# A mixer layer on one core: routing weights spread by DMA and multiplied in by GpSimd, score maxima woven in by fours

## The chip, the cores and the metric

The kernel runs on one core of one Trainium2 chip. The metric is the time of one execution on the device in microseconds; lower is better. Before the change it is 1653.61 us, the median of three runs (1653.0 to 1655.18).

## The reference

x has 8 sequences of 1024 tokens with 256 features. The layer normalizes x (no affine part), gives the result to two branches, and adds both to x:

```
xn  = layernorm(x)
out = x + attention(xn) + experts(xn)

attention: 16 heads of 16; heads 0..3 see every earlier token, heads 4..15 the last 64
    w = softmax(mask(q @ k.T * 16**-0.5));  ctx = w @ v;  out = ctx @ w_out + b_out

experts, once forward and once "inverse" (8 experts of rank 64 each), with Q and K projections of xn:
    xV = Q V;  yW = K W;  prod = xV * cumsum(yW over tokens)
    weights = softmax(gelu(Q @ r1.T + b1) @ r2.T + b2 + expert_bias)        # 8 weights per token
    out = (sum over experts of (prod * weights) @ U.T + weights @ b) / (position + 1)
out = (forward + alpha * inverse) @ W_O.T
```

All inputs and the output are float32. The product of three factors, `xV * weights * cumsum(yW)`, is what the change rearranges.

## The kernel before

**Work.** The 8 sequences are cut into 16 chunks of 512 tokens, `ch` = 0 to 15. Even chunks are the first half of a sequence, odd ones the second half, whose global heads see twice the keys. Features stand on the 128 partitions and tokens in the free dimension. Float32 matmuls are made from split operands: a value is a high part that TensorE takes, plus the rest (`XH`, `XL`; `CH`, `CL` for the running sums over tokens; `PH`, `PL` for the products; `WH`, `WL` for weights), so one product is three passes.

**Order.** A planner (`Plan`) writes one list of stages by hand-made rules. Each engine's program walks the whole list and issues its own part of each stage in that order, with semaphores between the engines; `uses=` gives a stage its turn on a PSUM bank or buffer. SP issues all DMAs, in the same order. A stage thus waits in every engine's queue behind all stages ahead of it in the list.

**The expert stage of a chunk.** Both branches together are eight blocks of 128 rows (two experts each), j = 0 to 7. For each block:

1. `x` (TensorE, line 587 through `mms`): six matmuls of 512 columns into bank 2. ScalarE copies bank 2 to `prod[:, j % 3]` (line 993).
2. `c`: the same from the running sums into bank 3.
3. `product`: TensorE spreads the routing weights of the two experts over 64 partitions each. It is one matmul of the 0/1 matrix `spread[:, j, :]` with `WT` (99 rows: the weights cut into three bfloat16 parts, by tokens) into bank 4 (line 701). VectorE multiplies `prod` by bank 4 (line 1273), then by bank 3 (line 1276). ScalarE rounds the result to `PH` (line 1003) and GpSimd subtracts it to get `PL` (line 1446).
4. `mix` (line 714): eight matmuls of 256 columns with `PH` and four with `PL`, into banks 0 and 1, which collect the output of the whole chunk. `open` (line 675) starts them with the bias terms.

`expert_groups` orders the groups: x(j+1), then c(j) with product(j), then mix(j-1). Into them `weave` sets the maxima of the attention scores, which the softmax of this chunk needs. `peak_groups` lists 12 local maxima (`lpeak`, one mask matmul at line 726 and eight small ones at line 732) and 10 or 26 global ones (`gpeak`, lines 743 and 746). It adds `found` (VectorE cuts the maxima into bfloat16 parts), `rows` (TensorE turns the local ones, ScalarE copies them out, SP stores and reloads them) and nine pieces of the next chunk's layernorm on VectorE. Each maximum is read from its bank by VectorE (lines 1197 and 1204). Before the change the list is cut into groups of two, and the maxima take turns on banks 5, 6 and 7.

**The stages behind it.** The local stage: scores of the twelve local heads, with the next chunk's transposes (`turn`), running sums (GpSimd, into `CH` and `CL`, from `rest`) and parts of q and k (through `rest` as well). The parts go out to DRAM and come back rearranged (`stacks`, local heads first, lines 1502 and 1523; global heads at line 1525). The global stage: scores of the four global heads, with the next chunk's x(0), c(0), router (`hidden`, `logits`), `gates` and `gate_parts`, where VectorE forms the weights `gate[:, 2]` (line 1255) and their three parts, and the values (`values`, then `vshift` by DMA). `weight_rows` turns the parts into `WT`. After it come x(1) and x(2) of the next chunk, around the turning of the context (`cparts`), then `finish`: 24 matmuls of the output projection (line 856), VectorE adds the residual in two halves (`xt`, line 1306) and SP stores the chunk (line 1560). SP then waits for that store before it loads the next residual (line 1494). Local scores take their bank by line 766, the first matmul behind the expert stage.

## Time and profile before

| | us |
|---|---|
| median of 3 runs | 1653.61 |
| the profiled execution | 1654.62 |
| its span, first to last instruction | 1652.9 |
| TensorE busy | 1563.5 |
| VectorE busy | 937.7 |
| ScalarE busy | 684.4 |
| GpSimd busy | 284.2 |

The profile is of one execution. Times within it are microseconds from the start of the span. Busy times of TensorE are modelled, since matmuls overlap in the array; a row's mean duration (0.39 us for a matmul of 512 columns) is thus longer than what it adds to a sequence (0.23 us), which the chain shows. The chain is the work that ended last, followed back step by step to what released it. DMA figures are the packets of the core's 16 DMA engines; the share of a queue is the packets' time over 16 engines times the stretch, and can pass 100% a little, where packets overlap. The granted TensorE clock was 0.996 of full speed.

### The profile page before, as it was taken

The numbers are of one execution on the slowest core, as the hardware profiler recorded it, in microseconds if no ns is written. First come the engines' busy times: TensorE is split into PE (matmuls) and PEld (weight loads), VectorE is DVE, ScalarE is ACT, GpSimd is POOL, SyncE is SP. The second block draws the span as 40 slices with busy tenths as digits, with TensorE's granted clock in tenths as the row PEclk, the third lists the DMA queues.
The fourth block names the chain that finished last, engine by engine and source line by source line (L and its number), as shares of the span: only waits on it lengthen the run. The fifth ranks groups of instructions, "written<-read, shape, count | busy, mean of one in ns | idle before, by whom it ended". The sixth has DMA issues, their size and how long they took to land.

```text
span 1652.9 us, 36914 instructions
## 1 busy us (share of the span) xinstructions
PE 1563.5 (95%) x15489; PEld 1112.8 (67%) x15489; DVE 937.7 (57%) x2048; ACT 684.4 (41%) x1224; POOL 284.2 (17%) x346
## 2 busy tenths in 40 slices
PE   5899999999999999999999999999999999999997
PEld 4576675767757676676757767576675767667674
DVE  6665672737537484564837567274763748447461
ACT  3426245261543517243362523626254351634425
POOL 2011121211112111121201212021111201112111
PEclk9999999999999999999999999999999999999999
DMA  8514417072350906218071350806326080530800
GB/s 207 63 31 88 80 34 123 10 117 51 76 89 4 151 15 104 61 38 130 4 122 45 77 91 21 125 21 106 62 64 100 4 139 27 96 69 23 132 4 14
DMA packets 128186, 116.48 MB, mean 70 GB/s; under 512 B 19251, under 2 KB 127668, under 8 KB 127972
## 3 DMA queue, kind: packets, MB, share of 16 engines
q1 hardware_dynamic: 128020, 114.12, 38.5%
q8 instruction: 122, 2.00, 0.6%
q14 instruction: 44, 0.36, 0.1%
HBM read 73.43 MB, written 34.34 MB: 65 GB/s over the span
## 4 chain that ended last, share of the span: by engine, by line
PE 76%; DVE 14%; ACT 5%; issue 4%; POOL 1%; DMA 0%; DVEq 0%; ACTq 0%; POOLq 0%
PE PS L587 33%; PE PS L714 8%; DVE block_peak L1204 4%; PE PS L793 3%; PE PS L825 3%; PE PS L732 3%; PE PS L856 3%; PE PS L766 3%; PE PS L807 3%; PE PS L772 3%; DVE prod L1273 2%; PE PS L726 2%; DVE prod L1276 2%; ACT HE L1029 2%; PE PS L746 2%
## 5 line engine op out<-in xcount | busy, mean ns | idle before, releaser
L1446 POOL TENSOR_TENSOR PL<-prod,PH 128x512 fp32r<-128x512 f32 x128 | 164.5, 1285 | 792.7 <-ACT PH L1003 792.7
L1003 ACT ACTIVATE PH<-prod 128x512 fp32r<-128x512 f32 x128 | 80.8, 631 | 428.8 <-DVE prod L1276 428.8
L587 PE MATMUL PS<-XH,WH 128*128 128x512 f32 x512 | 220.4, 430 | 4.5 <-DVE XL L1145 1.9
L587 PE MATMUL PS<-XH,WL 128*128 128x512 f32 x512 | 203.6, 398 | 0.0
L587 PE MATMUL PS<-XL,WH 128*128 128x512 f32 x512 | 203.2, 397 | 0.0
L1204 DVE TENSOR_REDUCE block_peak<-PS 128x4 f32<-128x512 f32 x288 | 186.9, 684 | 4.2 <-PE PS L746 4.2
L993 ACT ACTIVATE prod<-PS 128x512 f32<-128x512 f32 x128 | 76.3, 596 | 231.3 <-PE PS L587 220.3
L1029 ACT ACTIVATE HE<-PS 128x512 f32<-128x512 f32 (+1 forms) x320 | 159.7, 552 | 26.1 <-PE PS L807 23.5
L1197 DVE TENSOR_REDUCE peak<-PS 128x4 f32<-128x512 f32 x192 | 125.6, 685 | 41.0 <-PE PS L732 41.0
L1273 DVE TENSOR_TENSOR prod<-PS,prod 128x512 f32<-128x512 f32 x128 | 88.1, 689 | 104.6 <-PE PS L701 104.6
L714 PE MATMUL PS<-UH,PH 128*128 128x256 f32 x512 | 139.5, 306 | 0.0
L1439 POOL TENSOR_SCALAR_AFFINE_SELECT HE<-HE 128x256 f32<-128x256 f32 x128 | 50.7, 409 | 478.9 <-ACT HE L1029 476.4
L1286 DVE RECIPROCAL cinv<-PS 128x16 f32<-128x16 f32 x64 | 16.3, 254 | 205.2 <-PE PS L837 205.2
L714 PE MATMUL PS<-UL,PH 128*128 128x256 f32 x512 | 126.0, 280 | 0.0
L587 PE MATMUL PS<-CH,WH 128*128 128x512 f32 x256 | 109.2, 427 | 9.1 <-DVE prod L1276 9.0
L587 PEld LDWEIGHTS PS<-XH,WH 128*128 128x128 f32 x512 | 96.9, 189 | 26.6 <-DVE WL L1341 2.2
L1021 ACT ACTIVATE HE<-PS 128x512 f32<-128x512 f32 x192 | 104.6, 596 | 21.5 <-PE PS L772 21.5
L587 PEld LDWEIGHTS PS<-XH,WL 128*128 128x128 f32 x512 | 96.7, 189 | 23.1
L807 PE MATMUL PS<-area 99*128 99x256 bf16 (+1 forms) x640 | 100.4, 267 | 7.8 <-ACT HE L1029 3.9
L587 PEld LDWEIGHTS PS<-XL,WH 128*128 128x128 f32 x512 | 97.3, 190 | 14.6
L746 PE MATMUL PS<-area 96*128 96x128 bf16 x1152 | 100.8, 220 | 5.8 <-DVE block_peak L1204 4.9
L807 PEld LDWEIGHTS PS<-area 99*128 99x128 bf16 x640 | 41.8, 98 | 93.5 <-ACT HE L1029 56.9
(195 smaller groups left out, 3154.8 us busy)
## 6 DMA issues: line engine op xcount, KB each, us to landing
parts_d<-area SPq DMA_DIRECT2D x32, 768.0 KB, 5.1
area<-parts_d SPq DMA_DIRECT2D x128, 192.0 KB, 12.4
area<-parts_d SPq DMA_DIRECT2D x32, 576.0 KB, 12.5
tok<-in_L_attn_x_dram SPq DMA_DIRECT2D x16, 512.0 KB, 6.5
xt<-in_L_attn_x_dram SPq DMA_DIRECT2D x16, 512.0 KB, 3.9
out_dram<-xt SPq DMA_DIRECT2D x16, 512.0 KB, 3.7
area<-parts_d SPq DMA_DIRECT2D x96, 64.0 KB, 5.9
Vs<-Va SPq DMA_DIRECT2D x24, 204.0 KB, 7.6
```

What stands on the lines that cost most here:

```text
L587: ins = e.matmul(ps, a, b, start=first and k == 0, stop=last and k == n - 1, skip_group_check=True)
L714: ins = e.matmul(out_half(t), (PH, PL)[part][:, h, t * P:(t + 1) * P], u[:, j, :], start=False, stop=False, skip_group_check=True)
L746: ins = e.matmul(psum(i, lo=P * g, hi=P * (g + 1)), QS[0:G16, g, t * P:(t + 1) * P], KG[0:G16, g, j * P:(j + 1) * P], start=(g == 0 and no ...
L807: ins = e.matmul(psum(i, lo=HALF * a + lo, hi=HALF * (a + 1)), KG[0:KSTK, g, j * P:(j + 1) * P], QS[0:KSTK, g, half * HALF + lo:(half + 1) ...
L993: e.activation(prod[:, j % 3, :], psum(2), ACT.Copy).then_inc(bank_read[2])
L1003: e.activation(PH[:, h, :], prod[:, j % 3, :], ACT.Copy).then_inc(phi)
L1021: e.activation(HE[:, k, :], psum(i), ACT.Exp, scale=SCALE).then_inc(bank_read[i])
L1029: e.activation(two(HE[:, k, :], lo), two(psum(i), lo), ACT.Exp, scale=SCALE).then_inc(bank_read[i])
L1197: e.tensor_reduce(peak[:, t, NG + 4 * grp:NG + 4 * (grp + 1)], psum(i).rearrange("p (a k) -> p a k", a=4), AX_X, ALU.max).then_inc(bank_re ...
L1204: e.tensor_reduce(block_peak[ch % NC][:, t, :, j], psum(i).rearrange("p (a k) -> p a k", a=4), AX_X, ALU.max).then_inc(bank_read[i])
L1273: e.tensor_tensor(prod[:, r, :], psum(4), prod[:, r, :], ALU.mult).then_inc(bank_read[4])
L1446: e.tensor_tensor(PL[:, j % 2, :], prod[:, j % 3, :], PH[:, j % 2, :].bitcast(F32), ALU.subtract).then_inc(plo)
```

## The change

The weights no longer go through TensorE's spread. `gate_parts` gets a VectorE transpose of 32x32 blocks of `gate[:, 2:4]` into `weights_t`. SP writes it to DRAM as `weights_d` (16 rows of 512 tokens, float32) in four DMAs. For each block j a stage `wide` reads two rows of it, each 64 times, into one of three buffers of 128 x 512 float32 (two of them are `rest`). A stage `weigh` on GpSimd multiplies `prod` by it, before `product`. wide(j + 3) is issued behind weigh(j). Bank 4 so becomes free of the spread, and the maxima take turns on banks 4 to 7 and are cut into groups of four. `spread`, its selects and its memset are gone. `WT` stays for the bias terms.

```diff
@@ peak_use
-        return f"bank{(5, 6, 7)[turns['peak'] % 3]}"
+        return f"bank{4 + turns['peak'] % 4}"
@@ expert_groups
-                order.append([(add_x, ch, j + 1, part) for part in range(2)])
+                order.append([(add_x, ch, j + 1, part) for part in range(2)] + [(add_weigh, ch, j + 1)])
@@ planner
     def add_product(ch, j):
-        add("product", ch, j, uses=["bank4"])
+        add("product", ch, j)
+    def add_weigh(ch, j):
+        add("weigh", ch, j)
+        if j + WIDE < 2 * KB:
+            add_wide(ch, j + WIDE)
+    def add_wide(ch, j):
+        add("wide", ch, j, uses=[f"wide{j % WIDE}"])
+    def add_gate_parts(ch):
+        add("gate_parts", ch)
+        for j in range(WIDE):
+            add_wide(ch, j)
@@ peak_groups
-        return [order[n] + (order[n + 1] if n + 1 < len(order) else []) for n in range(0, len(order), 2)]
+        return [[stage for group in order[n:n + 4] for stage in group] for n in range(0, len(order), 4)]
@@ behind the global stage (weigh(0), (1), (2) of the next chunk around x(1), cparts, x(2))
+            add_weigh(ch + 1, 0)
             run([(add_x, ch + 1, 1, part) for part in range(2)])
+            add_weigh(ch + 1, 1)
...
             run([(add_x, ch + 1, 2, part) for part in range(2)])
+            add_weigh(ch + 1, 2)
@@ TensorE
-                elif kind == "product":
-                    e.matmul(psum(4), spread[:, j, :], WT[:, :], start=True, stop=True).then_inc(w_ps)
@@ VectorE, turn (rest is also a buffer of wide)
+                        q.wait_ge(weighed, nth("weigh", ch - 1, 6 + k))
@@ VectorE, gate_parts
+                    q.wait_ge(weights_out, 16 * 4 * ch)
+                    e.transpose(weights_t[:, :].rearrange("p (t w k) -> p t w k", t=T, w=2),
+                                gate[:, 2:4].rearrange("p w t k -> p t w k")).then_inc(weights_turned)
+                    q.wait_ge(weights_turned, ch + 1)
@@ VectorE, product
-                    q.wait_ge(w_ps, nth(*stage))
-                    e.tensor_tensor(prod[:, r, :], psum(4), prod[:, r, :], ALU.mult).then_inc(bank_read[4])
+                    q.wait_ge(weighed, nth("weigh", ch, j))
                     q.wait_ge(c_ps, nth(*stage))
                     e.tensor_tensor(prod[:, r, :], psum(3), prod[:, r, :], ALU.mult).then_inc(bank_read[3])
@@ GpSimd
+                elif kind == "weigh":
+                    q.wait_ge(bank_read[2], use("bank2", "x", ch, j, 0))
+                    q.wait_ge(wide_in[j % WIDE], 16 * use(f"wide{j % WIDE}", "wide", ch, j))
+                    e.tensor_tensor(prod[:, j % 3, :], prod[:, j % 3, :], wide[j % WIDE], ALU.mult).then_inc(weighed)
@@ SP
+                elif kind == "gate_parts":
+                    q.wait_ge(weights_turned, ch + 1)
...
+                    for g in range(4):
+                        e.dma_start(weights_d.rearrange("k (t g r) -> g k t r", t=T, g=4)[g],
+                                    weights_t[32 * g:32 * g + 2 * KE, :].rearrange("k (t r) -> k t r", t=T)).then_inc(weights_out, 16)
+                elif kind == "wide":
+                    q.wait_ge(weights_out, 16 * 4 * (ch + 1))
+                    if j >= WIDE:
+                        q.wait_ge(weighed, nth("weigh", ch, j - WIDE))
...
+                    e.dma_start(wide[j % WIDE], weights_d[2 * j:2 * j + 2, :].unsqueeze(1).to_broadcast([2, R, C])).then_inc(wide_in[j % WIDE], 16)
```

## Rows read from the trace of the kernel before

**Rows 1.** The page: part 1, and the first line of part 4 (the chain).

```profile
PE 1563.5 (95%) x15489; PEld 1112.8 (67%) x15489; DVE 937.7 (57%) x2048; ACT 684.4 (41%) x1224; POOL 284.2 (17%) x346
...
PE 76%; DVE 14%; ACT 5%; issue 4%; POOL 1%; DMA 0%; DVEq 0%; ACTq 0%; POOLq 0%
```

**Rows 2.** Busy time by stretch, one pair of chunks: us, then busy us (instructions) of each engine, clock, DMA share, GB/s.

```profile
370.81:567.97 197.16, 189.99 (x1920) 135.75 (x1921) 112.76 (x248) 83.18 (x149) 34.68 (x41) 1.00 0.39 70
```

**Rows 3.** The chain through a second half: start us, us, what.

```profile
373.88 0.26 DVE xt L1306
...
374.49 0.69 DVE prod L1273
...
377.62 0.23 PE PS L701
...
385.87 0.32 PE PS L726
386.19 0.34 PE PS L732 x8
386.54 1.60 PE PS L587 x6
...
393.28 1.32 DVE stats L1118 x4
...
404.88 0.45 PE PS L746 x8
...
407.25 1.45 PE PS L587 x6
...
422.46 0.39 PE PS L766
```

**Rows 4.** The chain through a first half.

```profile
283.20 0.26 DVE xt L1306
...
325.94 0.38 PE PS L766
```

**Rows 5.** Groups by line: busy us, mean ns, then idle before.

```profile
L1446 POOL TENSOR_TENSOR PL<-prod,PH 128x512 fp32r<-128x512 f32 x128 | 164.5, 1285 | 792.7 <-ACT PH L1003 792.7
...
L1273 DVE TENSOR_TENSOR prod<-PS,prod 128x512 f32<-128x512 f32 x128 | 88.1, 689 | 104.6 <-PE PS L701 104.6
```

**Rows 6.** DMA packets, 340 to 346 us (parts_d<-area, one store of 768 KB).

```profile
DMA packets 784, 0.79 MB, mean 131 GB/s; under 512 B 16, under 2 KB 784, under 8 KB 784
...
q1 hardware_dynamic: 784, 0.79, 39.0%
```

**Rows 7.** DMA packets, 394 to 395.6 us (peak_d_local<-peak_f alone, 36 KB).

```profile
DMA packets 48, 0.04 MB, mean 23 GB/s; under 512 B 12, under 2 KB 48, under 8 KB 48
```

**Rows 8.** DMA packets, 395.6 to 400 us (area<-peak_d_local alone, 36 KB).

```profile
DMA packets 7, 0.05 MB, mean 12 GB/s; under 512 B 3, under 2 KB 3, under 8 KB 3
...
q1 hardware_dynamic: 6, 0.04, 3.5%
```

**Rows 9.** DMA packets, 4 to 7 us (the first loads).

```profile
q1 hardware_dynamic: 542, 0.93, 80.8%
```

**Rows 10.** SP's DMA issues in order of time: start us, us, what.

```profile
394.34 0.33 SPq L1553 DMA_DIRECT2D peak_d_local<-peak_f  x1
395.81 0.26 SPq L1555 DMA_DIRECT2D area<-peak_d_local  x1
```

**Rows 11.** VectorE in order of time, gates before a second half.

```profile
359.31 0.22 DVE L1255 TENSOR_TENSOR gate<-gate,gsum 128x64 f32<-128x64 f32 x1
```

**Rows 12.** DMA queue, 360 to 366 us.

```profile
q1 hardware_dynamic: 788, 0.77, 117.8%
```

**Rows 13.** VectorE in order of time, gates before a first half.

```profile
457.02 0.23 DVE L1255 TENSOR_TENSOR gate<-gate,gsum 128x64 f32<-128x64 f32 x1
```

**Rows 14.** Busy time by stretch, the last full one of that DMA load.

```profile
464.00:466.00 2.00, 2.00 (x21) 1.44 (x21) 0.00 (x0) 1.02 (x3) 0.77 (x2) 1.00 1.19 121
```

**Rows 15.** Busy time by stretch, chunk 0.

```profile
85.00:90.00 5.00, 5.00 (x48) 2.92 (x47) 3.36 (x6) 1.54 (x3) 0.24 (x1) 1.00 0.81 158
```

More of the change, by code:

```diff
@@ L316, in mixer_layer @@
         add_on("fold_u", n, uses=[fold_use()])
-    add("gate_parts", 0)
+    add_gate_parts(0)
     for part in range(2):
         add_x(0, 0, part)
+    add_weigh(0, 0)
     for part in range(2):
@@ L359, in mixer_layer @@
             order = order[1:]
-            side = [[(add_gates, ch + 1)], [(add, "gate_parts", ch + 1)]] + [[]] * (2 * (ch % NC))
+            side = [[(add_gates, ch + 1)], [(add_gate_parts, ch + 1)]] + [[]] * (2 * (ch % NC))
             side += [[(add_values, ch + 1, 0)], [(add_values, ch + 1, 1)]]
@@ L391, in mixer_layer @@
         bias_rows = sb("bias_rows", [KSTK, D], BF16)
-        spread = sb("spread", [KSTK, 2 * KB, P], BF16)
         W2 = sb("W2", [P, DB, KE])
@@ L428, in mixer_layer @@
         rest = sb("rest", [P, 2, C])
+        weights_t = sb("weights_t", [P, T * 32])
+        wide = [rest[:, 0, :], rest[:, 1, :], sb("wide2", [P, C])[:, :]]
         carry = sb("carry", [P, DB])
@@ L511, in mixer_layer @@
         logits_ps, gate_max, gate_exp, gate_split, gate_turned = (sem(n) for n in ("logits_ps", "gate_max", "gate_exp", "gate_split", "gate_turned"))
-        x_ps, c_ps, w_ps, phi, plo = (sem(n) for n in ("x_ps", "c_ps", "w_ps", "phi", "plo"))
+        x_ps, c_ps, phi, plo = (sem(n) for n in ("x_ps", "c_ps", "phi", "plo"))
+        weights_turned, weights_out, weighed = (sem(n) for n in ("weights_turned", "weights_out", "weighed"))
+        wide_in = [sem(f"wide{i}_in") for i in range(WIDE)]
         lpeaks_ps, gpeaks_ps, lscores_ps, gscores_ps, ctx_turned, ctx_hi, out_ps = (
@@ L695, in tensor_program @@
                         ins.then_inc(c_ps)
-                elif kind == "product":
-                    ch, j = key
-                    q.wait_ge(bank_read[7], use("bank7", "weight_rows", ch))
-                    take(4, *stage)
-                    e.matmul(psum(4), spread[:, j, :], WT[:, :], start=True, stop=True).then_inc(w_ps)
                 elif kind == "mix":
@@ L1105, in vector_program @@
                         e.memset(view, 0.0).then_inc(blank)
-                    for view in (ident, ident_b, peak_mask_l, peak_mask_g, spread, mask_l):
+                    for view in (ident, ident_b, peak_mask_l, peak_mask_g, mask_l):
                         e.memset(view[:], 0.0).then_inc(cleared)
@@ L1270, in vector_program @@
                     r = j % 3
-                    q.wait_ge(bank_read[2], use("bank2", "x", ch, j, 0))
-                    q.wait_ge(w_ps, nth(*stage))
-                    e.tensor_tensor(prod[:, r, :], psum(4), prod[:, r, :], ALU.mult).then_inc(bank_read[4])
-                    q.wait_ge(bank_read[4], use("bank4", *stage))
+                    q.wait_ge(weighed, nth("weigh", ch, j))
                     q.wait_ge(c_ps, nth(*stage))
@@ L1408, in gpsimd_program @@
                     select(peak_mask_l[0:64, 1, :], [[1, P]], -WINDOW, 0, after=7)
-                    for n, first in enumerate((0, 3 * HD, 5 * HD)):
-                        view = spread[:, :, :].rearrange("r j (a m) -> r (j a) m", a=2)
-                        select(view, [[-1, 4 * KB], [0, R]], -first, 1, ALU.not_equal, 1.0, after=8 + n if n else 0)
                     select(mask_l[:, :], [[-1, WINDOW]], 0, 1)
-                    select(mask_l[:, :], [[1, WINDOW]], WINDOW, -1, after=12)
+                    select(mask_l[:, :], [[1, WINDOW]], WINDOW, -1, after=9)
                     e.iota(positions[:, :], pattern=[[P, ST]], base=1, channel_multiplier=1).then_inc(selected)
@@ L1555, in sync_program @@
                     e.dma_start(QS[G16:KSTK, lo:lo + n, :], peak_d[which].rearrange("(a h) t -> a h t", h=n)).then_inc(peak_in[which], 16)
+                elif kind == "gate_parts":
+                    ch, = key
+                    q.wait_ge(weights_turned, ch + 1)
+                    for i in range(WIDE):
+                        q.wait_ge(wide_in[i], 16 * (use(f"wide{i}", "wide", ch, i) - 1))
+                    for g in range(4):
+                        e.dma_start(weights_d.rearrange("k (t g r) -> g k t r", t=T, g=4)[g],
+                                    weights_t[32 * g:32 * g + 2 * KE, :].rearrange("k (t r) -> k t r", t=T)).then_inc(weights_out, 16)
+                elif kind == "wide":
+                    ch, j = key
+                    q.wait_ge(weights_out, 16 * 4 * (ch + 1))
+                    if j >= WIDE:
+                        q.wait_ge(weighed, nth("weigh", ch, j - WIDE))
+                    elif j == 2:
+                        q.wait_ge(weighed, nth("weigh", ch - 1, 5))
+                    else:
+                        q.wait_ge(part3, nth("parts", ch, 0, DB - 1))
+                        q.wait_ge(clo, DB * (ch + 1))
+                        if ch == 0:
+                            q.wait_ge(bias_in, 16 * 15)
+                    e.dma_start(wide[j % WIDE], weights_d[2 * j:2 * j + 2, :].unsqueeze(1).to_broadcast([2, R, C])).then_inc(wide_in[j % WIDE], 16)
                 elif kind == "finish":
```

9 lines of the change are left out of this document (5 added, 4 removed).

## The prediction

> **What bounds the kernel now.** First the page's busy table and its chain: TensorE is busy for 95% of the span and carries 76% of the chain, VectorE 14% [rows 1]. Then the busy time by stretch: chunks come in pairs, a first and a second half of a sequence, and each pair takes 197.2 us with 190 us of TensorE, the DMA engines 0.39 busy on the mean [rows 2]. Then the chain through one chunk. F is the moment at which the last matmul of `finish` of the chunk before has ended. In a second half the chain leaves F at 373.9, goes over VectorE (`xt`, then `prod` twice) back to TensorE, where each L701 (the spread) costs 0.23, and reaches the first local score at 422.5, F+48.6 [rows 3]. In a first half it takes from 283.2 to 325.9, F+42.8 [rows 4]. This "expert stage", eight experts woven with the maxima, is what the change touches; the local and global stages behind it stay. So TensorE bounds, with VectorE close behind it in the second halves. DMA has 0% of the page's chain [rows 1], so its rows have to be looked up for themselves: the change makes eight DMAs per chunk a condition of the products.
>
> **What goes.** 128 spread matmuls at 0.23 on the chain [rows 3]: 29.4 us of TensorE, 1.84 per chunk. 128 VectorE multiplications of 0.69 (88 us) [rows 5], which lie partly in the chain: at a chunk's start one stands between `xt` and c(1) [rows 3]. Bursts of four on four banks switch weights less often and spare some 0.3 to 0.6 us per chunk (six matmuls after local maxima take 1.60, after global ones 1.45, else 1.40 [rows 3], and half as many such places remain; back-to-back bursts pay 0.1 of it). The memset and three selects at the start are beside the first loads and cost nothing.
>
> **What comes on engines.** 128 GpSimd multiplications, priced by the subtraction of the same three operands, 1.285 [rows 5]. GpSimd then works 2.6 us per expert of 5 to 6 us, and is idle otherwise in this stage. The order counts though: weigh(j+1) stands in GpSimd's queue before the subtraction PL(j), and mix(j) waits for PL(j). If weigh(j+1) waits for its rows, so does mix(j). One VectorE transpose per chunk lies in the gate stage, where VectorE idles: nothing. `rows` now takes bank 4 amid a burst; in a second half it waits for VectorE's read of a maximum that stands behind the layernorm moments (1.32 for their first part, 1.9 with all of it [rows 3]), 2.6 us with the maxima themselves; in a first half the next maximum waits for ScalarE's copy of `rows`, 0.85 (both estimates).
>
> **What comes on the DMA engines, the step that decides.** Each `wide` writes 128 partitions of 2 KB, 256 KB, from a source whose outermost count is 2 (two rows, each repeated 64 times). How many engines carry one DMA can be read from its completion packets. The store of the parts, 128 partitions, shows 784 packets in its window, 768 of data and 16 under 512 B [rows 6]. The store of the local maxima, 36 rows, shows 48 packets, of which 12 are small [rows 7]. The load behind it, 36 rows taken as 3 by 12, shows 6 packets on the kernel's queue, 3 small and 3 of data [rows 8]. So 128 went over 16 engines, 36 over 12, an outermost 3 over 3. No row shows a DMA whose sides differ, as a `wide` has 2 at its source and 128 at its target: by the source it goes over 2 engines, by the target over 16. I take 2, since a part that goes to one engine must be whole on both sides, and keep 16 as a rival. The Trainium skill ("DMA: Bandwidth & Descriptors", Why a DMA increments its semaphore by 16 and not by 1) has a rule for it: the largest count up to 16 that divides the slowest dimension of both patterns, always on the lowest-numbered engines. By that rule a `wide` has 2, and always the same two; the trace's 16, 12 and 3 agree with it, and no run here shows the mixed case yet.
>
> The price of one `wide` on its two engines is 131 KB per engine. One engine moved 0.79 MB/(0.390 x 6.0 us x 16) = 21.1 GB/s in packets of 1 KB [rows 6], 0.93/(0.808 x 3.0 x 16) = 24.0 in the first loads, with packets of 3 KB among them [rows 9], and 37 KB/(0.035 x 4.4 x 16) = 15 in the 12 KB packets into single partitions [rows 8]. That gives 6.2, 5.5 and 8.7 us. A packet of 2 KB is nearest to the first two: I take 23 GB/s, 5.7 us, and keep 5.2 to 8.7. Eight are 46 us per chunk on those two engines, in a stage that takes 42.8 or 48.6, and each engine serves its DMAs in order, so that the others stand in the same line. A landing costs 1.5 us from issue on top: the store of the maxima is issued at 394.3 and the load that waits for it at 395.8 [rows 10].
>
> The line on the two engines, second half (F = 373.9). The weights are ready after L1255, at 359.5 [rows 11]; the DMA engines are full with the local stacks until 366 (117.8% busy) [rows 12], and the four weight DMAs stand behind them. So the first `wide` starts at F-6.4, three end at F+10.7. Vs and the global stacks (1.18 MB, 74 KB per engine at 21 GB/s, 3.5 us) then stand behind them: F+14.2. wide 3 to 5, issued after weigh 0 to 2: F+31.3. The store of the output stands behind wide 5 in SP's program, which waits for weigh(2): F+32.8, landed F+34.3. SP then waits for that landing before the next residual load, and wide 6 and 7 stand behind this load in the program: load to F+36.7, wide 7 to F+48.1, landed F+49.6, weigh(7) F+50.9, PL(6) F+52.2, mix(6) F+53.7. Before: 48.6. Loss 5.1.
> First half (F = 480.3). The weights are ready at 457.2 [rows 13] and land once the local stacks are through, at 466 (1.19 busy until then [rows 14]): three wides from F-13.0 to F+4.1, Vs and stacks F+7.5, wide 5 F+24.6, store landed F+27.6, load F+30.0, wide 7 F+41.4, landed F+42.9, mix(6) ends F+47.0. Before: 42.8. Loss 4.2.
> Seven such pairs (chunks 1 to 14): 7 x 9.3 = 65 us. Chunk 0: its DMA engines are busy until about 90 (0.81 from 85 on [rows 15]); eight wides end at 136.1, mix(6) at 141.7, where now the stage ends at 128.8: 13. Chunk 15 has a third of its experts in the local stage and loses nothing. The sum is 78 us on the profiled execution's 1654.6 (span 1652.9 and 1.7 around it; the median of the runs is 1653.6, 1.0 lower): 1733. TensorE's savings are inside this: it waits them out.
>
> **Rivals.** (1) All 16 engines carry a `wide`, and it lands 2.3 us after its issue (262 KB at 16 x 21 GB/s, and 1.5 on top), long before its product; then TensorE bounds on. Its work in a second half, by the pieces of rows 3: 19 groups of x, c and mix at 1.40, `open` 0.54, spreads 1.84, 12 local maxima (0.66 each, 0.34 and 0.32) with their switches 8.5, 26 global ones (0.225 each, a mask for four) with theirs 7.5, `rows` 0.2: 45.2, so 3.4 of the 48.6 are waits for VectorE. The spreads and these waits go, 0.65 of switches too, and 2.6 for `rows` comes: 3.3 faster. First half: 41.1 of work and 1.7 of waits; 1.84, 0.5 and 1.6 go, 1.05 comes: 2.9. Seven pairs: 43 us, 1611; with the spreads alone 1625. For it: the trace has room (0.39); against it: the counts of rows 7 and 8. (2) Two engines, but 26 GB/s each (5.0 us): 0.7 x 8 = 5.6 less per chunk than in the sum, over 15 chunks 84: 1733 becomes 1649, and 1620 to 1650 if the line of DMAs is also shorter than I count. The point at which the sign turns is thus 5.0 us per `wide`. For it: 24.0 of rows 9 is a mean over many DMAs, with gaps; against it: that the rows read have been written just before, all 64 times from the same place. (3) 15 GB/s, as in rows 8: 3 us more for each of eight in 15 chunks, 360: 2093; 1913 for half of that. For it: it is the one load over few engines that the trace has; against it: its packets are six times longer and go to one partition each. (4) GpSimd and VectorE block one another. Both already run side by side 128 times with 1.285 and 0.69 as unchanged means [rows 5]; I give it nothing of its own.
>
> **How the numbers follow.** Forecast (1733, own range 1655 to 1860) 0.69; rival 1 0.14; rival 2 0.08; rival 3 0.09. A change under 0.2% (3 us) could not be told from none here. Faster: rival 1 and three quarters of rival 2, 0.20; same 0.03; slower 0.77. The range 1630 to 1890 leaves out rival 1 and the far part of rival 3.
>
> **What would show it.** The small packets per `wide`: 2, not 16; issue to landing 7 us alone and 10 to 25 in the stage; GpSimd's weigh waiting for DMAs, above all 6 and 7; TensorE waiting for PL at L714, its busy share under 92%, the maxima of VectorE long done; an expert stage of 54 and 47 us. Wrong if a `wide` lands in 3 to 4 us with 16 small packets: then stages of 45.3 and 39.9 and rival 1's time.

## The result and the profile after

The changed kernel takes 1852.9 us (median of 4 runs, 1847.2 to 1854.9); the kernel before, run beside it, 1654.4. The ratio is 1.119, 95% interval 1.117 to 1.121: slower by 198 us, where 78 were forecast. The direction held; the size did not.

The page of the changed kernel, part 1, the TensorE clock and the chain, beside [rows 1]:

```profile
PE 1604.6 (87%) x15361; PEld 1156.5 (62%) x15361; DVE 871.6 (47%) x1935; ACT 681.2 (37%) x1224; POOL 441.2 (24%) x471
...
PEclk9989899998989889898998989989899998989989
...
q1 hardware_dynamic: 149780, 148.20, 38.0%
...
PE 55%; DMA 25%; DVE 10%; SPq 2%; ACT 2%; POOL 2%; issue 2%; POOLq 0%; ACTq 0%; DVEq 0%
...
out_dram<-xt SPq DMA_DIRECT2D x16, 512.0 KB, 15.4
```

TensorE's share of the chain fell from 76% to 55%, and DMA's rose from 0 to 25%. The chain's next line puts 16% of the span on `wide` and 8% on the store of the weights. TensorE is busy 1604.6 us. The instructions of before less the 128 spreads make 1563.5 - 29.4 = 1534.1. The surplus is 70.5 us; most of it is the same work at a lower clock, as e6 and e18 below show. The output's store lands 15.4 us after its issue; before it took 3.7.

One pair of chunks, beside [rows 2]; 222.0 us where it was 197.2, at a mean granted clock of 0.92:

```profile
531.60:753.60 222.00, 195.92 (x1903) 141.02 (x1902) 104.58 (x234) 82.82 (x148) 54.74 (x57) 0.92 0.39 81
```

The DMA share is 0.39 in both. No mean over sixteen engines shows two that are full. What does is the packet count, in the way of [rows 6 to 8]. Here is the queue from 656 to 662 us, where only the transfers of `wide` move bytes and one of them ends (the output's store is issued in it, and its packets of 1 KB come later):

```profile
DMA packets 145, 0.29 MB, mean 49 GB/s; under 512 B 2, under 2 KB 2, under 8 KB 145
...
q1 hardware_dynamic: 145, 0.29, 13.0%
```

There are two packets under 512 B, and the share is 13.0% of sixteen engines, which is 2.08 of them: a `wide` runs on two engines. The pages' counts of packets under 512 B say the same of all chunks together: 24627 here and 28467 in e1, 3840 more, which is 256 transfers with 16 for 128 with 2. In the whole trace the packets of 2 KB have a median of 84 ns and a mean of 94, that is 5.4 to 6.0 us for the 64 on each engine.

GpSimd's multiplications through a second half (F = 631.5), in order of time, with the two subtractions behind the third. In brackets is what GpSimd waited for, and how long:

```profile
638.37 1.26 POOL L1461 TENSOR_TENSOR prod<-prod,rest 128x512 f32<-128x512 f32 x1 [16.68 <-DMA rest<-weights_d]
644.45 1.26 POOL L1461 TENSOR_TENSOR prod<-prod,rest 128x512 f32<-128x512 f32 x1 [4.82 <-DMA rest<-weights_d]
652.27 1.26 POOL L1461 TENSOR_TENSOR prod<-prod,wide 128x512 f32<-128x512 f32 x1 [6.56 <-DMA wide<-weights_d]
653.49 2.50 POOL L1466 TENSOR_TENSOR PL<-prod,PH 128x512 fp32r<-128x512 f32 x2
661.41 1.28 POOL L1461 TENSOR_TENSOR prod<-prod,rest 128x512 f32<-128x512 f32 x1 [5.42 <-DMA rest<-weights_d]
...
671.29 1.28 POOL L1461 TENSOR_TENSOR prod<-prod,rest 128x512 f32<-128x512 f32 x1 [5.11 <-ACT prod L1009]
...
690.89 1.30 POOL L1461 TENSOR_TENSOR prod<-prod,rest 128x512 f32<-128x512 f32 x1 [4.30 <-DMA rest<-weights_d]
```

weigh(0) runs at F+6.9 and weigh(2) at F+20.8. Directly behind weigh(2) come two subtractions, PL(0) and PL(1). The list has weigh(0), (1) and (2) ahead of the first `product`, so PL(0), and with it mix(0), stands in GpSimd's queue behind the third multiplication. For weigh(4) and (5) GpSimd waits for ScalarE, for weigh(7) again for a transfer. SyncE's issues of the same stretch show why the first comes so late:

```profile
605.05 6.83 SPq L1543 DMA_DIRECT2D area<-parts_d  x8
617.52 2.54 SPq L1583 DMA_DIRECT2D weights_d<-weights_t  x4
630.65 1.10 SPq L1598 DMA_DIRECT2D rest<-weights_d  x2
631.79 2.79 SPq L1598 DMA_DIRECT2D wide<-weights_d  x1
634.68 5.53 SPq L1556 DMA_DIRECT2D Vs<-Va  x1
...
641.46 7.42 SPq L1545 DMA_DIRECT2D area<-parts_d  x8
648.92 4.53 SPq L1598 DMA_DIRECT2D rest<-weights_d  x2
...
657.88 5.20 SPq L1603 DMA_DIRECT2D out_dram<-xt  x1
673.26 0.40 SPq L1514 DMA_DIRECT2D xt<-in_L_attn_x_dram  x1
```

The local stacks are issued from 605.1 and the four small stores of the weights from 617.5; the stores land at 630.6, F-0.9. With two-engine transfers under way, single issues take 2.8 to 5.5 us of SyncE where [rows 10] have 0.3.

TensorE over that stretch. The columns are: us, then busy us (instructions) of PE, PEld, DVE, ACT and POOL, granted clock, DMA share, GB/s:

```profile
625.00:636.00 11.00, 8.84 (x78) 6.61 (x76) 2.89 (x5) 2.17 (x4) 0.00 (x0) 1.00 0.43 55
636.00:641.00 5.00, 0.59 (x2) 0.50 (x2) 1.34 (x3) 0.61 (x1) 1.26 (x1) 0.50 0.14 48
641.00:646.00 5.00, 5.00 (x28) 2.77 (x26) 2.00 (x4) 0.02 (x1) 1.26 (x1) 0.50 0.60 151
...
651.00:656.00 5.00, 1.19 (x5) 1.20 (x6) 0.00 (x0) 0.00 (x0) 3.71 (x3) 0.50 0.15 46
656.00:661.00 5.00, 5.00 (x34) 2.72 (x32) 1.21 (x2) 0.60 (x1) 0.00 (x0) 0.61 0.13 49
```

TensorE stood still for 6.3 us ahead of c(1) and for 4.3 ahead of the part of mix(0) that takes PL(0), and from 636 to 656 the clock is granted at 0.50, the 1.2 GHz level. Its waits, summed over the kernel, each with the number of times and the longest:

```profile
PE PS L731 <- POOL PL L1466: 98.3, 15, 7.5
PE PS L610 <- DVE prod L1294: 55.4, 16, 9.1
PE PS L774 <- DVE block_peak L1221: 22.1, 8, 3.0
```

The prediction had the first kind (PL, late through `wide`) and the third (`rows` on bank 4: 2.76 us each, estimated 2.6). In the pair shown, the expert stage of the second half takes 64.4 us (forecast 53.7), that of the first half 52.1 (forecast 47.0, [rows 4] 42.8). The 48.6 that the prediction read for a second half before [rows 3] goes to the second matmul of line 766. To the first, as the 64.4 is measured, it is 47.8 (TensorE in order of time, F = 373.9):

```profile
421.66 0.39 PE L766 MATMUL PS<-mask_l,ident_b 128*128 128x512 bf16 x1
```

The two stages thus lose 16.6 and 9.3 us, 25.9 a pair, where the windows have 24.8.

### The profile page after: what moved, and what is told of

Same layout as the page of the kernel before. It is cut to its first block, busy times and chain, and to the rows that moved or that the text cites. A ratio compares the mean times of both kernels' runs of the same rounds, so it can differ in the third digit from the quotient of the medians.

```text
span 1853.2 us, 36905 instructions
## 1 busy us (share of the span) xinstructions
PE 1604.6 (87%) x15361; PEld 1156.5 (62%) x15361; DVE 871.6 (47%) x1935; ACT 681.2 (37%) x1224; POOL 441.2 (24%) x471
## 2 busy tenths in 40 slices
DMA packets 149947, 150.56 MB, mean 81 GB/s; under 512 B 24627, under 2 KB 133044, under 8 KB 149732
## 4 chain that ended last, share of the span: by engine, by line
PE 55%; DMA 25%; DVE 10%; SPq 2%; ACT 2%; POOL 2%; issue 2%; POOLq 0%; ACTq 0%; DVEq 0%
PE PS L610 25%; DMA wide<-weights_d 16%; DMA weights_d<-weights_t 8%; PE PS L731 8%; DVE block_peak L1221 4%; PE PS L810 3%; PE PS L789 2%; PE PS L783 2%; PE PS L749 2%; PE PS L743 2%; PE PS L763 2%; PE PS L928 2%; SPq L1583 2%; DVE tok L1154 1%; PE PS L854 1%
## 5 line engine op out<-in xcount | busy, mean ns | idle before, releaser
L1461 POOL TENSOR_TENSOR prod<-prod,rest 128x512 f32<-128x512 f32 x96 | 122.9, 1280 | 517.7 <-DMA rest<-weights_d 387.5
L610 PE MATMUL PS<-XH,WH 128*128 128x512 f32 x512 | 226.5, 442 | 4.5 <-DVE XL L1161 1.9
L610 PE MATMUL PS<-XH,WL 128*128 128x512 f32 x512 | 212.6, 415 | 0.0
L610 PE MATMUL PS<-XL,WH 128*128 128x512 f32 x512 | 211.9, 414 | 0.0
L731 PE MATMUL PS<-UH,PL 128*128 128x256 f32 x512 | 89.4, 300 | 98.3 <-POOL PL L1466 98.3
L610 PE MATMUL PS<-CH,WH 128*128 128x512 f32 x256 | 118.4, 462 | 55.4 <-DVE prod L1294 55.4
L731 PEld LDWEIGHTS PS<-UH,PL 128*128 128x128 f32 x512 | 74.9, 204 | 101.4 <-POOL PL L1466 101.4
L731 PE MATMUL PS<-UH,PH 128*128 128x256 f32 x512 | 132.9, 293 | 0.0
L610 PEld LDWEIGHTS PS<-XL,WH 128*128 128x128 f32 x512 | 102.7, 201 | 15.7
L610 PE MATMUL PS<-CL,WH 128*128 128x512 f32 x256 | 108.2, 423 | 0.0
## 6 DMA issues: line engine op xcount, KB each, us to landing
out_dram<-xt SPq DMA_DIRECT2D x16, 512.0 KB, 15.4
```

The lines of the kernel that those rows point to most:

```text
L610: ins = e.matmul(ps, a, b, start=first and k == 0, stop=last and k == n - 1, skip_group_check=True)
L731: ins = e.matmul(out_half(t), (PH, PL)[part][:, h, t * P:(t + 1) * P], u[:, j, :], start=False, stop=False, skip_group_check=True)
L1461: e.tensor_tensor(prod[:, j % 3, :], prod[:, j % 3, :], wide[j % WIDE], ALU.mult).then_inc(weighed)
```

## The experiments

Two theories at first. The two-engine transfers cost the time, by the line on their rings as the prediction laid it out, only longer. Against it: the way over two engines (GpSimd, then VectorE), the maxima on four banks, or TensorE's clock carry a good part by themselves. All ratios are to the kernel before, run beside each. "Maxima" gives how they are woven in (pairs or fours) and on how many banks; "`wide` on" is the number of DMA engines of one transfer.

| kernel | `wide` on | maxima | us | ratio, 95% |
|---|---|---|---|---|
| before | – | pairs, 3 banks | 1654 | 1 |
| the change | 2 | fours, 4 | 1852.9 | 1.119 [1.117, 1.121] |
| e1 | 16 | fours, 4 | 1661.3 | 1.004 [1.002, 1.006] |
| e2 | 16 | pairs, 3 | 1652.5 | 0.999 [0.998, 1.001] |
| e3 | 2 | pairs, 3 | 1837.2 | 1.110 [1.107, 1.113] |
| e4 | – | fours, 3 | 1685.3 | 1.019 [1.017, 1.021] |
| e8 | 16 | fours, 3 | 1684.1 | 1.018 [1.016, 1.020] |
| e10 | 16 | pairs, 4 | 1676.0 | 1.015 [1.012, 1.019] |
| e14 | 4 | fours, 4 | 1720.3 | 1.042 [1.038, 1.045] |
| e15 | 16 first 3, 2 last 5 | fours, 4 | 1661.5 | 1.005 [1.003, 1.007] |
| e16 | 2 first 3, 16 last 5 | fours, 4 | 1860.9 | 1.125 [1.123, 1.128] |
| e18 | 16, TensorE filled | pairs, 3 | 1641.6 | 0.992 [0.990, 0.993] |

### The two parts of the change, taken apart

e1, `wide` on sixteen engines; nothing else moves but the semaphore's count (32 for 16):

```diff
-e.dma_start(wide[j % WIDE], weights_d[2 * j:2 * j + 2, :].unsqueeze(1).to_broadcast([2, R, C]))
+for h in range(2):
+    e.dma_start(wide[j % WIDE][R * h:R * (h + 1), :], weights_d[2 * j + h:2 * j + h + 1, :].to_broadcast([R, C]))
```

> The changed kernel with each `wide` transfer cut into two, one for each of its two source rows, so that the outermost dimension of each is 64 destination partitions and no longer 2 source rows; same bytes, same waits. If the loss comes from the transfers running on two of the sixteen DMA engines, this kernel lands a `wide` in about a microsecond and falls to what the first rival of the prediction gave, 1611 us, or up to 10 us above, as the stores of the weights still land only at the end of `finish`. If what costs is the way of the product over GpSimd (VectorE and GpSimd in a row where one engine was) or the maxima on four banks, it stays above 1750. If it is the clock of TensorE alone, which fell in the waits on those transfers, it also goes, as the waits go: this kernel does not tell that apart.

1661.3 us. The two engines are worth 191.6 of the 198 us, so the way over GpSimd is not what costs them. But 1661 is not the 1611 of the prediction's first rival.

e2 puts the maxima back on top of e1, e3 on top of the change:

```diff
-return f"bank{4 + turns['peak'] % 4}"
+return f"bank{(5, 6, 7)[turns['peak'] % 3]}"
-return [[stage for group in order[n:n + 4] for stage in group] for n in range(0, len(order), 4)]
+return [order[n] + (order[n + 1] if n + 1 < len(order) else []) for n in range(0, len(order), 2)]
```

> The kernel with the `wide` transfers on sixteen engines, and the maxima woven in by pairs on banks 5, 6 and 7, as before the change: the spreading alone. The prediction's sum for this was 1625 us, that is 14 us more than with the fours. If the fours and their wait on bank 4 cost something rather than save it, this one is at or under the time of its neighbour with the fours.

> The changed kernel as it is with two-engine transfers, but the maxima by pairs on banks 5, 6 and 7: the first half of the change alone. If the transfers set the time, the order of the maxima changes little: 1853 us within 15. If the maxima on four banks have a good part in the loss of 198 us, it falls below 1800.

1652.5 and 1837.2. Fours on four banks cost 9 us with sixteen engines and 16 with two, where the prediction's 1625 and 1611 had them save 14. The spreading alone on sixteen engines equals the kernel before; I had given 1625. The tie is a balance: in e2's profiled run the stage of a first half takes 39.7 us (before 42.8) and that of a second half 50.3 (before 47.8). Here and below, such a pair of numbers without a chunk is the mean of the seven first or second halves among chunks 1 to 14, by the timelines of TensorE.

e4 has the last two lines of that diff reversed in the kernel before, which makes its pairs fours; e8 does the same to e2. e10 has e2 on banks 4 to 7.

> The kernel before, with the maxima woven in by fours, still on banks 5, 6 and 7 (bank 4 is taken by the spread weights there): the second half of the change without its fourth bank. Four maxima in a row on three banks make TensorE wait for VectorE's reduction once in each group: I expect 1654 us plus 0 to 15. A rival, that longer stretches of one kind of work save changes in the order and so TensorE time, gives 1645.

> The spreading on sixteen engines with the maxima by fours on banks 5, 6 and 7, without the fourth bank. On the kernel before, this step cost 31 us, and TensorE's wait for the maxima's reductions 37 us. If the fourth bank is what makes fours bearable, this gives 1652 plus 25 to 35; if the cost on the kernel before came from VectorE being busier there (128 products more), under 1665.

> The spreading on sixteen engines, maxima by pairs, but on banks 4 to 7: the fourth bank without the fours. With fours on four banks the time was 1661, with pairs on three 1652.5, with fours on three 1684. If bank 4 costs because `rows` uses it too (TensorE waited 22 us there in second halves and 5.5 in first), this gives 1665 to 1675. If the fours are what costs and a fourth bank only ever helps, it gives 1652 or a few us less.

Fours on three banks cost 31 us, both on the kernel before and on e2. e4 came out above its expectation. These are TensorE's waits there for the reductions of the maxima, which were 4.9 and 0.6 us in the kernel before:

```profile
PE PS L746 <- DVE block_peak L1204: 36.9, 46, 1.5
...
PE PS L726 <- DVE peak L1197: 9.2, 17, 0.6
```

The fourth bank alone costs 23 (e10), where TensorE waits 17.5 us ahead of `rows` for VectorE's read of bank 4, and 5.5 behind `rows`. The two together cost 9. So the fourth bank takes most of the fours' wait away, and on four banks the fours are 15 us faster than pairs (e1 against e10). `rows` on the same bank is the wait that stays, 22.1 and 5.5 us in e1; that it is the whole price was not shown. e7 tried to take that wait away too, by putting `rows` two maxima later in second halves:

```diff
-gpeaks[2].append((add_rows, ch, 0))
+gpeaks[4 if c else 2].append((add_rows, ch, 0))
```

> The whole change with `wide` on sixteen engines (1661.3 us), and in second halves the `rows` of the local maxima two maxima later, so that the bank 4 that it takes was last used three maxima ahead and not one. TensorE's 8 waits there, 22.1 us in all, should go: 1639 to 1645 us. If VectorE, which is late with the maxima, is itself the bound of that stretch, the wait only moves to the next maximum and the time stays at 1661.

1658.0 us, with 10 runs spread from 1651 to 1669, so the gain of 3 on e1 is not shown. In its profiled run, the longest of the ten, the wait for VectorE was gone and that of the next user of bank 4 for ScalarE's copy had grown:

```profile
PE PS L763 <- ACT peak_f L1031: 23.1, 16, 2.4
```

In e1 the same row has 5.5 us (8 times, at most 0.7). The wait moved, as the second sentence of the expectation had it, though not to VectorE.

### Where in the chunk the two engines cost

e14 keeps the packets but spreads each `wide` over four engines (e1's two DMAs, with the source as `to_broadcast([4, R // 4, C])`):

> The whole change with each `wide` cut in two, with an outermost dimension of four in each: the packets are the same 128 of 2 KB, on four DMA engines instead of two, 32 on each. By 84 to 94 ns a packet that is 2.7 to 3.0 us a transfer, and 22 to 24 us a chunk on these rings instead of 43 to 48. If the loss comes from how long a `wide` fills its rings, it halves or better against sixteen engines (1661): 1670 to 1720. If what matters is only that a few rings are more loaded than the rest and everything that spans all sixteen waits for them, it is still above 1750.

1720.3 us: 59 above sixteen engines, where two have 192. Twice the engines leave a third of the loss. e15 and e16 split the eight transfers of a chunk by `j < 3` and `j >= 3`:

```diff
+for h in range(2 if j < 3 else 1):
+    if j < 3: (e1's transfer of one row)
+    else: (the change's transfer of both rows)
```

> The whole change with the first three `wide` of each chunk on sixteen engines and the five others on two. TensorE's long waits in the changed kernel are those for the first two products of a chunk (98 us at mix(0) and 55 at c(1)), and the first three `wide` are what is late there. If the loss of 192 us against sixteen engines is theirs, this gives 1661 plus 20 to 50: 1695. If it is the line of the five others that sets the stage, 1800 or more.

> The counterpart: the first three `wide` of each chunk on two engines, the five others on sixteen. If the first three carry the loss, this gives 1853 less 10 to 50: 1820. If it is the line of the five others, 1720 or less. Were the two parts independent, the gains of this kernel and of its counterpart would add up to 192 us; if the losses overlap, so that either group alone is enough to be late, they add up to less.

1661.5 and 1860.9 us, and both expectations had the first three carry less. This is the sharpest pair of the study: with the first three on sixteen engines the loss is gone to the last microsecond, though five of eight still run on two; with only the first three on two it is all there. That e16 is 8 us above the changed kernel is not explained. GpSimd in e15, in a second half with F = 577.9:

```profile
580.59 2.64 POOL L1466 TENSOR_TENSOR prod<-prod,rest 128x512 f32<-128x512 f32 x2 [12.53 <-DMA rest<-weights_d]
583.19 1.30 POOL L1466 TENSOR_TENSOR prod<-prod,wide 128x512 f32<-128x512 f32 x1
...
595.02 1.29 POOL L1466 TENSOR_TENSOR prod<-prod,rest 128x512 f32<-128x512 f32 x1 [7.44 <-DMA rest<-weights_d]
...
604.04 1.28 POOL L1466 TENSOR_TENSOR prod<-prod,rest 128x512 f32<-128x512 f32 x1 [6.50 <-ACT prod L1014]
...
624.26 1.29 POOL L1466 TENSOR_TENSOR prod<-prod,rest 128x512 f32<-128x512 f32 x1 [4.04 <-DMA rest<-weights_d]
```

weigh(2) is at F+5.3 rather than F+20.8, and the stage ends at F+51.6. That is 46 us behind weigh(2); in the changed kernel the end is 43.6 behind it. The rest of a second half takes its 44 to 46 us whichever engines carry transfers 3 to 7, and 43.6 in e16 too. The reason that the third transfer counts, and not only the first, stands in GpSimd's queue: PL(0) waits behind weigh(2). No run put PL(0) ahead of it, so what that would give back is not known. e12 says the same of the piece of the line that I had counted with most care, the residual's load between `wide` 5 and 6. It moves this load behind `wide` 7:

> The changed kernel with the load of the residual (which waits for the landing of the output's store, 15.4 us after its issue as it stands behind two-engine transfers) moved behind the last `wide` of the chunk in SyncE's queue. In the profiled chunk SyncE sat in that wait from 657.9 to 673.3 while `wide` 6 could have been issued at about 661. If that wait is on the path, each second half gains 5 to 8 us and each first half some: 1853 less 50, so 1803 within 15. If the two engines are busy in that time anyway with the output's store and `wide` 5, so that `wide` 6 would land no earlier, 1845 or more.

1850.4 us (ratio 1.119 [1.117, 1.121]): nothing. The 15 us that SyncE spends from the issue of that store to its landing are off the path.

### Why the first product is late

Three ways to get the small stores of the weights in before the stacks' bytes. e5 lets ScalarE issue them, e17 GpSimd, on their own queues; e9 holds all four local stacks of Q back behind the first three `wide`, e13 only the three small ones. All four are made from e2; e11 is e9's edit in the changed kernel.

```diff
 elif kind == "weights_out":              # e5: in ScalarE's program, e17: in GpSimd's
+    for g in range(4):
+        e.dma_start(weights_d...[g], weights_t[32 * g:32 * g + 2 * KE, :]...).then_inc(weights_out, 16)
```
```diff
-side = [[(add_gates, ch + 1)], [(add_gate_parts, ch + 1)]] + ...
+side = [[(add_gates, ch + 1)], [(add_gate_parts, ch + 1), (add, "stacks", ch + 1, "local", 0)]] + ...
```

> The spreading alone, `wide` on sixteen engines, maxima by pairs; now ScalarE issues the four small stores of the weights on its own queue, so that they do not stand behind the local stacks on SyncE's. The trace with SyncE shows them landing only at the end of `finish`, GpSimd waits 184 us in all for `wide`, TensorE 31 us (8 times) for the product behind it, and the granted clock drops after these waits. If the late weights are why the spreading alone gave 1652.5 us and not the 1625 of the prediction's rival, this kernel gives 1625 within 8, and TensorE's waits for the product fall from 31 us to under 8. If the small stores are slow in themselves or the engines are full of the stacks whatever the queue, it stays at 1650.

> The spreading alone, `wide` on sixteen engines, maxima by pairs; of the local stacks only the four transfers of K stand ahead of the stores of the weights in SyncE's queue, the four of Q come behind the first three `wide`. With ScalarE as the issuer TensorE's wait for the late product went from 31 us to 5, but the issuing itself held ScalarE and TensorE waited 42 us for the exponentials. Here nobody but SyncE issues. If the small stores are late because eight stacks stand ahead of them in the same rings, they now land 8 to 10 us earlier, the wait goes, and the time is 1625 within 8. If they are late for another reason, it stays at 1652.

> The spreading alone, sixteen engines, maxima by pairs; only the three small local stacks of Q (192 KB each, a quarter of the local bytes) are held back behind the stores of the weights and the first three `wide`. With all four of Q held back the product came in time but TensorE waited 47 us for the local stacks instead, 5.9 in each second half. Now the stores should land some 5 us ahead of the end of `finish` rather than at it, and the local stacks about as TensorE needs them: TensorE's wait for the product (31 us) goes down to under 10 and that for the stacks to under 15, time 1628 within 10. If a microsecond gained on one side is always lost on the other, 1650 or more.

> The spreading alone, sixteen engines, maxima by pairs, and the four small stores of the weights issued by GpSimd on its own queue; the stacks stay where they were. From ScalarE this took TensorE's wait for the product from 31 us to 5 but made TensorE wait 42 us for the exponentials, 3 to 3.8 each time, as the issuing held ScalarE. GpSimd is idle 73% of the time; TensorE waits for it only at the masks on the diagonal, 9 us in all. If no other engine's work stands behind the issuing, both waits are gone and the time is 1615 to 1630, under both kernels. If GpSimd's issuing is slow or holds up its masks by 3 us in each chunk, 1650 to 1670 again.

> The changed kernel (two-engine `wide`) with the four local stacks of Q behind the stores of the weights and the first three `wide`. The prediction had the stores land 7 us ahead of the end of `finish` in a second half and 13 in a first; the trace has 0.9 and 11. If this delay is passed on through the whole line of transfers, it is worth 6 us in each of 8 second halves and 2 in each first: 60 us, so 1793, within 15. If the first three products are late but the line catches up at the end of the stage, which ScalarE and the residual's load hold anyway, 1840 or more.

e5 1668.4, e9 1677.9, e13 1669.0, e17 1653.8, e11 1954.4 us. None of them gave 1625. The store's median from issue to landing, first in e2, then in e17, e13 and e9 (columns: times, KB, us):

```profile
weights_d<-weights_t SPq DMA_DIRECT2D x64, 8.0 KB, 10.2
```
```profile
weights_d<-weights_t POOLq DMA_DIRECT2D x64, 8.0 KB, 10.1
```
```profile
weights_d<-weights_t SPq DMA_DIRECT2D x64, 8.0 KB, 5.5
```
```profile
weights_d<-weights_t SPq DMA_DIRECT2D x64, 8.0 KB, 2.3
```

From GpSimd's queue the small stores land no earlier (10.1 us for 10.2); with a quarter of the local bytes held back they take 5.5, with half 2.3. So they are late because the sixteen engines are full of the stacks, and not because they stand in SyncE's queue. In e5 the landing fell to 7.6, but its stores were issued later into the same load: in one profiled chunk of e2, e17 and e5 the reads that wait for the stores are issued 18.4, 18.1 and 18.3 us behind the last local stack, so the stores landed at the same moment of the load. And the four issues held ScalarE:

```profile
564.00 3.53 ACTq L994 DMA_DIRECT2D weights_d<-weights_t  x4
567.63 1.36 ACT L1056 ACTIVATE HE<-PS 128x512 f32<-128x512 f32 x3 [3.19 <-issue]
569.21 0.39 ACT L1056 ACTIVATE HE<-PS 128x256 f32<-128x256 f32 x1 [0.21 <-PE PS L826]
```

TensorE waited 41.6 us there for the exponentials. In e9 and e13 the product's wait is gone (one of 7 us stays, where it was 8 times) and the stacks are late in its place:

```profile
PE PS L746 <- DMA area<-parts_d: 46.9, 8, 6.8
```
```profile
PE PS L747 <- DMA area<-parts_d: 40.7, 8, 6.0
```

So the local maxima, which come soon after F, leave the stacks that they read no slack. In e11, where the three `wide` ahead of the stacks of Q are on two engines, TensorE waits 260 us for the stacks, up to 21.9 at a time, and the time is 101 us above the changed kernel. The late store is thus the price of moving the weights through memory at that moment; none of the three queues made it earlier.

### What TensorE's clock costs

e6 fills the long waits of the changed kernel with matmuls whose result is overwritten, e18 those of e2 (14 ahead of c(1) in second halves):

```diff
+elif kind == "fill":
+    take(2, *stage)
+    for k in range(24 if n == 0 else 18 if ch % NC else 28):      # e18: range(14)
+        ins = e.matmul(psum(2), WH[:, 0, 0:P], XH[:, 0, :], start=True, stop=True, skip_group_check=True)
+    ins.then_inc(bank_read[2])
```

> The changed kernel with idle matmuls (into bank 2 while it is free, their result is overwritten) in TensorE's long waits: 24 ahead of c(1) in each second half, and 28 or 18 (first or second half) ahead of the second part of mix(0). They are some 6, 4 and 5 us at the full clock, less than the waits of 7.1, 4.3 and 6.3 us. Nothing else moves. TensorE is busy 1612 us in the changed kernel where the instructions before, less the 128 spreads, make 1534: 78 us more, all at a granted clock of one half. If these 78 us add to the time, this kernel gives 1775. If the transfers set the time of the stage whatever TensorE's clock is, it stays at 1853. Since some of the slow stretch lies ahead of a further wait for a transfer, my expectation is between: 1810 within 20.

> The spreading alone, sixteen engines, maxima by pairs, and 14 idle matmuls (about 3 us) ahead of c(1) in each second half, where TensorE waits 3.5 to 6.2 us for the product. If the clock that falls after this wait costs all of TensorE's surplus of busy time (14 us), the time is 1638; if part of it is hidden, 1645. Both would be under the kernel before (1654). If the clock falls anyway or costs nothing here, 1652, and no variant of the change tried here is faster than the kernel before.

The expectation of e6 gives the changed kernel's busy time and surplus as 1612 and 78 us; by the page they are 1604.6 and 70.5. e6: 1829.2 us, 24 under the changed kernel. The windows of e6 over the same waits, a second half with F = 625.3:

```profile
636.00:641.00 5.00, 5.00 (x53) 3.39 (x51) 2.07 (x4) 0.63 (x1) 1.28 (x1) 1.00 0.56 150
641.00:646.00 5.00, 3.19 (x14) 2.24 (x12) 1.51 (x3) 0.00 (x0) 0.37 (x1) 1.00 0.34 93
646.00:651.00 5.00, 2.84 (x9) 2.45 (x10) 0.00 (x0) 0.00 (x0) 3.34 (x3) 0.69 0.13 46
651.00:656.00 5.00, 5.00 (x48) 3.10 (x47) 3.54 (x5) 0.60 (x1) 1.30 (x1) 0.97 0.13 49
```

The clock stays at 1.00 where it was 0.50, except behind the 4 us that the filling left open. TensorE is busy 1678.7 us, of which the fillers 128.8, so 1549.9: the surplus over 1534.1 fell from 70.5 to 15.8. Of these 54.7 us, 24 came back as time, and not where the windows above lie: the stage of a first half fell from 51.9 to 48.3 us, while that of a second half stayed at 64.4, with the clock at 1.00 where it had been 0.50. There the landing of the first three transfers and the work behind the third took as long at either clock.

e18: 1641.6 us, 10.9 under e2 and 0.8% under the kernel before (ratio 0.992 [0.990, 0.993]). Its page and its fillers:

```profile
PE 1563.7 (95%) x15473; PEld 1130.2 (69%) x15473; DVE 871.6 (53%) x1935; ACT 683.3 (42%) x1224; POOL 443.2 (27%) x471
```
```profile
L729 PE MATMUL PS<-XH,WH 128*128 128x512 f32 x112 | 29.8, 419 | 0.0
```

1563.7 less 29.8 is 1533.9: the surplus, 14.9 us in e2, is gone. TensorE's waits for the product shrank from 31.0 to 8.8, since the fillers now stand in them. The stage of a second half fell from 50.3 to 48.2 us, that of a first half, where nothing was filled, stayed at 39.7. It is the one kernel here that is faster than the kernel before.

## Why the prediction was wrong in its size

**Held.** The bound and the carrier: a `wide` runs on two engines (2 small packets, 13.0% of sixteen), and rival 1 and its sixteen engines fall. By the Trainium skill's rule ("DMA: Bandwidth & Descriptors", Why a DMA increments its semaphore by 16 and not by 1) it should be two; the trace agrees. e1 and e14, where the same bytes go as two transfers each, with outermost counts of 64 and 4, give 192 and 133 us back. The rate, nearly: 5.7 us in the forecast, 5.4 by the median packet; in the burst of three 6.7 (issued from 630.7, weigh(2) at 652.3, less 1.5 for the landing), inside the 5.2 to 8.7. Its slow part falls where Vs and the global stacks ran beside it, and not behind it as the line had them: the two engines moved 24 to 25 packets of 2 KB a microsecond from 632 to 636, and 14 to 21 from 640 to 650. The price of `rows`: 2.76 us for 2.6, and 0.69 for 0.85. Rival 4: GpSimd's mean stays 1.28 and VectorE's 0.69.

**The step that failed** is "The line on the two engines", in three ways. First its start and its first three transfers: "the first `wide` starts at F-6.4, three end at F+10.7". The stores of the weights landed at F-0.9, since the stacks filled the engines until F-3.5 and not until 366, F-8 [rows 12], and the three took 20 us rather than 17.1. With 1.5 for the landing, weigh(2) was forecast at F+12.2 and F+5.6 in the two halves; it ran at F+20.8 and F+10.3. Of these 13.3 us a pair, 7.5 are the later start and 5.8 the slower burst. In seven pairs they make 93 us.

Second, what the stage waits for. I let its end be set by the landing of `wide` 7, after a line over residual and store. e15 has five transfers on two engines at no cost, and e12 takes the residual's wait off that line at no gain. What sets the end is the third product: in the changed kernel the work behind weigh(2) takes 43.6 us in the second half shown and 41.8 in the first (F+20.8 to F+64.4; F+10.3 to F+52.1), and 46.3 in e15's second half (F+5.3 to F+51.6). In first halves 3 us of it hang on the clock: with the waits filled (e6) it is 38.4. With the forecast's own weigh(2) this gives 55.8 and 47.4 where the line gave 53.7 and 47.0: close, so the wrong tail did not show, which is luck. It is 2.5 us a pair, 18 us in seven pairs.

Third, the ends of the series. "Chunk 15 [...] loses nothing", but its first three transfers are as late as any: its stage took 55.6 us where it took 41.9 before, 13.7 more. Chunk 0 lost 9.5 (138.3 for 128.8) where 13 were forecast. In all 93 + 18 + 13.7 - 3.5 = 121, where 120 us were missed; left out are the 0.8 us a pair of the misread row and about as much by which the rest of a pair was shorter.

**The sum, as measured.** Spreading on sixteen engines: -2 (e2). Fours on four banks: +9 (e1). The first three transfers on two engines: +192 (e1 against the change, with e15 and e16 for the place). The last five: 0. Of the 192, the clock is 24 as far as e6 filled the waits, and the prediction did not have it at all. It said of TensorE's savings "it waits them out"; in fact TensorE also ran at the lower level behind its long waits.

**Rival 1's numbers** (1625 alone, 1611 with the fours) were wrong by 27 and 50. They are also not made of the same terms: 1625 is the 1654 less the 29.4 us of the spreads with every wait kept, while 1611 takes the waits for VectorE off too. In e1 the first half took 40.2 us against 39.9 forecast. The second took 51.9 against 45.3; the stores land at about F there, and the clock falls behind the wait: 31 us of waits in e2 and 14.9 of surplus busy time. e18 gives 11 back; how much of the rest is the late landing could not be priced, since each way to an earlier landing made something else late. Of the fours the prediction had the price of `rows` but not the wait for the reductions, which is the 31 us on three banks. Its own terms, 1.15 us a pair saved in switches and 3.65 paid for `rows`, make the fours cost some 17 us, not save 14; on four banks they cost 9.

## What to carry to other kernels

A transfer on few engines is dear where a wait stands open for it, and free where it runs ahead of its reader: find out which of a series are on the path, and spread those. Look also at what stands in the queue behind the instruction that waits; here the first block's mix hung on the third block's weights. Before counting on a small store, look at what the DMA engines carry at that moment; the issuing queue changed nothing, the bytes in flight did. A wait of some 4 us on TensorE can cost more than itself, for the clock is lower behind it. Filling it with idle matmuls gave 11 us of 1652 back in e18, and nothing in the second halves of e6, where a further wait stood behind.

## What the runs showed of the hardware

- The granted clock fell to the 1.2 GHz level behind TensorE's waits of 3.5 us (e2) to 7.1 us (the changed kernel) and came back later in the stage. Behind a wait of 2.2 us it was 0.68 over 5 us in e1 and 1.00 in e15. In e18, with 14 matmuls ahead of the wait's end, the surplus of busy time vanished.
- Behind two-engine transfers, one DMA issue held SyncE for up to 5.5 us (Vs at 634.7), against 0.66 for the same line in e2. Four issues of 8 KB while the engines were full took ScalarE 3.5 us (e5), SyncE 2.5 (e2) and GpSimd 2.0 (e17).
- The packets of 2 KB took 84 ns in the median on two, four and sixteen engines alike (means 94, 105 and 108), though the 64 reads of a row come from one place in memory.
